# A deformable convolution's sampling stage on TensorE: transposes as products with the unit matrix, and every product on tiles of 64 columns

## The reference, cut to what matters

```python
def deform_conv2d(x, offset, weight, bias, pad=PAD):
    ...
    val = gather(y0, x0, (1 - dy) * (1 - dx)) + gather(y0, x0 + 1, (1 - dy) * dx) \
        + gather(y0 + 1, x0, dy * (1 - dx)) + gather(y0 + 1, x0 + 1, dy * dx)
    patches = val.reshape(Bx, C, KK, Hx, Wx)
    out = jnp.einsum('bikhw,oik->bohw', patches, weight.reshape(Cout, Cin, KK))
    return out + bias[None, :, None, None]
f_w = deform_conv2d(xr, off_w, w_dcnw, b_dcnw)
f_h = deform_conv2d(xr, off_h, w_dcnh, b_dcnh)
f_avg = (f_w + f_h).mean(axis=(2, 3), keepdims=True)
```

## Time and profile before

| what | before |
|---|---|
| median of 3 runs | 12,407.22 us |
| the profiled execution: time / span | 12,423.67 / 12,421.6 us |
| sampling stage on TensorE | 563 to 7,577 us of the span |
| TensorE busy in the span | 93% |
| VectorE, ScalarE, GpSimd busy in the span | 83%, 83%, 48% |

### The profile page before, as it was taken

One profiled execution on the slowest core, in us unless ns is written; L12 is line 12 of the kernel. 1 busy time (PEld: TensorE's weight loads), 2 busy tenths in 40 slices (PEclk: granted clock), 3 DMA queues, 4 the chain that ended last, 5 costly groups with the idle time before them and its releaser, 6 DMA issues. The chain is left out here.

```text
span 12421.6 us, 338253 instructions
## 1 busy us (share of the span) xinstructions
PE 11555.8 (93%) x133056; PEld 8928.9 (72%) x133056; DVE 10330.4 (83%) x13907; ACT 10361.2 (83%) x10330; POOL 5958.3 (48%) x3910
## 2 busy tenths in 40 slices
PE   7699999999999999999999999880699899999999
PEld 4599999999999999999999996430533355555555
DVE  5588888888888888888888886799878788888888
ACT  3499899899998998989989885397768899899988
POOL 0155554455444545445454451033300388888887
PEclk9899999999999999999999997895899899999999
DMA  6688888888888888888888888444644333333332
GB/s 181 164 209 206 208 205 203 204 206 208 204 204 201 208 206 207 206 200 208 206 207 205 202 206 210 140 155 139 178 130 159 127 99 108 102 100 107 99 103 85
DMA packets 850969, 2144.79 MB, mean 173 GB/s; under 512 B 108322, under 2 KB 447184, under 8 KB 707168
## 3 DMA queue, kind: packets, MB, share of 16 engines
q1 hardware_dynamic: 833904, 2090.65, 63.7%
q10 hardware_dynamic: 15120, 30.71, 0.7%
q0 software_dynamic: 384, 1.79, 0.0%
HBM read 1827.33 MB, written 295.56 MB: 171 GB/s over the span
## 5 line engine op out<-in xcount | busy, mean ns | idle before, releaser
L831 PE MATMUL dc_p<-dc_t 96*64 96x108 f32 x103896 | 5162.5, 257 | 85.9 <-issue 44.9
L831 PEld LDWEIGHTS dc_p<-dc_t 96*64 96x64 f32 x103896 | 4847.6, 136 | 353.6 <-issue 351.7
L900 POOL TENSOR_TENSOR dc_t<-dc_t 128x486 f32<-128x486 f32 x2885 | 3169.6, 1099 | 3525.6 <-DVEq L990 2344.8
L972 DVE TENSOR_TENSOR dc_t<-dc_p,dc_t 128x972 f32<-128x972 f32 x2886 | 3367.5, 1167 | 976.0 <-DVEq L970 880.4
L779 ACT ACTIVATE dc_t<-dc_t 96x2304 f32<-96x2304 f32 x1447 | 3191.8, 2206 | 222.3 <-ACTq L778 219.0
L784 ACT ACTIVATE dc_t<-dc_t 96x2304 f32<-96x2304 f32 x1446 | 3049.7, 2109 | 0.0
L2481 DVE TENSOR_TENSOR_SCAN ms_t<-ms_t,ms_p 128x512 f32<-128x512 f32 x1728 | 2128.5, 1271 | 282.9 <-PE ms_p L2423 203.5
L2397 POOL TENSOR_TENSOR ms_t<-ms_t 128x1536 f32<-128x1536 f32 x576 | 1987.9, 3457 | 503.5 <-DVE ms_t L2481 499.7
L2433 PE MATMUL ms_p<-ms_t,top_t 128*128 128x512 f32 x3456 | 1774.7, 596 | 0.0
L2423 PEld LDWEIGHTS ms_p<-top_t,ms_t 128*128 128x128 f32 x6912 | 849.7, 141 | 967.6 <-issue 693.1
L872 PE MATMUL dc_p<-dc_t 128*128 128x180 f32 (+1 forms) x7488 | 1537.0, 337 | 0.6 <-PEq L867 0.3
(11 more groups left out here) (256 smaller groups left out, 9864.2 us busy)
## 6 DMA issues: line engine op xcount, KB each, us to landing
dc_t<-sxd SPq DMA_DIRECT2D x1447, 864.0 KB, 5.9
ms_t<-bcd SPq DMA_DIRECT2D x576, 256.0 KB, 3.3
dc_t<-xrT SPq DMA_DIRECT2D x145, 540.0 KB, 9.0
kvd<-wk_t SPq DMA_DIRECT2D x18, 1536.0 KB, 5.1
szd<-mi_t SPq DMA_DIRECT2D x36, 768.0 KB, 4.4
xvd<-mi_t SPq DMA_DIRECT2D x36, 768.0 KB, 4.8
dld<-mi_t SPq DMA_DIRECT2D x36, 768.0 KB, 3.4
ms_t<-dld SPq DMA_DIRECT2D x36, 768.0 KB, 6.7
```

The source lines that it names most:

```text
L831: ins = e.matmul(PT[j % 2][o:o + 64, t // 3, (t % 3) * WIN * CG:(t % 3 + 1) * WIN * CG], HX[:, m // 2 % RP, m % 2, t * 128 + o:t * 128 + o ...
L900: e.tensor_tensor(ZH[:, n % 4, :, :], z[:, :, 0:HALF], z[:, :, HALF:2 * HALF], ALU.add)\
L972: e.tensor_tensor(Zt[:, n % 4, :].rearrange("p (b m i) -> p b m i", b=3, i=CG), PT[n % 2][:, :, 0:3 * WIN * CG].rearrange("p b (m i) -> p ...
```

## The change

Both transposes (L859, L840) become ordinary matmuls: the data is now the stationary operand, 64 columns at a time, at column 0 or 64 of the array, and the unit matrix (128 columns) is the moving one. The convolution's matmul (L872) is split into two of 64 stationary columns in the same way, each against the same 180 moving columns. So that 64 columns are always there, `VA` is padded from 1,620 to 1,664 columns (zeroed once) and `ACC` from 180 to 218; the transposed pieces of `ACC` are then 128 columns from 0 and from 90 (they were 90 from each), of which 90 rows are used as before. VectorE's two copies of the last three chunks become one.

```diff
-        VA = p.sb([128, 2, NG * LEN])
+        VA = p.sb([128, 2, NCK * 128])
-        ACC = p.sb([128, NRB, 2, CM])
+        ACC = p.sb([128, NRB, 2, CM + 38])
...
                 def turn_sum(i, conv):
                     for h in range(2):
-                        ins = e.transpose(PR[0:HM, (2 + h) * 128:(3 + h) * 128], ACC[:, i, conv, h * HM:(h + 1) * HM],
-                                          k.ident[:, :])
+                        for o in (0, 64):
+                            ins = e.matmul(PR[o:o + 64, (2 + h) * 128:(3 + h) * 128],
+                                           ACC[:, i, conv, h * HM + o:h * HM + o + 64], k.ident[:, :],
+                                           start=True, stop=True, tile_position=(0, o))
...
                         for u, c in enumerate(pieces[g]):
-                            o = min(128, NG * LEN - 128 * c)
-                            ins = e.transpose(PR[0:o, u * 128:(u + 1) * 128],
-                                              VA[:, n // NG % 2, 128 * c:128 * c + o], k.ident[:, :])
+                            for o in (0, 64):
+                                ins = e.matmul(PR[o:o + 64, u * 128:(u + 1) * 128],
+                                               VA[:, n // NG % 2, 128 * c + o:128 * c + o + 64], k.ident[:, :],
+                                               start=True, stop=True, tile_position=(0, o))
...
                         for u, c in enumerate(pieces[g]):
-                            o = min(128, NG * LEN - 128 * c)
-                            ins = e.matmul(PF[:, conv * CM:(conv + 1) * CM], VT[0:o, n // 2 % 2, u, :],
-                                           WD[0:o, c, conv, :], start=(c == 0), stop=(c == NCK - 1),
-                                           skip_group_check=True)
+                            kr = min(128, NG * LEN - 128 * c)
+                            for o in (0, 64):
+                                ins = e.matmul(PF[o:o + 64, conv * CM:(conv + 1) * CM], VT[0:kr, n // 2 % 2, u, o:o + 64],
+                                               WD[0:kr, c, conv, :], start=(c == 0), stop=(c == NCK - 1),
+                                               skip_group_check=True, tile_position=(0, o))
...
+                e.memset(VA[:, :, NG * LEN:NCK * 128], 0.0)
...
-                    full = sum(128 * (c + 1) <= NG * LEN for c in pieces[g])
-                    ins = e.tensor_copy(VT[:, n // 2 % 2, 0:full, :].rearrange("p u x -> p (u x)"), PR[:, 0:full * 128])
-                    if full < len(pieces[g]):
-                        o = NG * LEN % 128
-                        ins = e.tensor_copy(VT[0:o, n // 2 % 2, full, :], PR[0:o, full * 128:(full + 1) * 128])
-                    ins.then_inc(s_vt, 1)
+                    m = len(pieces[g])
+                    e.tensor_copy(VT[:, n // 2 % 2, 0:m, :].rearrange("p u x -> p (u x)"), PR[:, 0:m * 128]).then_inc(s_vt, 1)
```

More of the change, by code:

```diff
@@ L905, in keep @@
                     e.wait_ge(s_cr[i % 2], 32).then_inc(s_cr[i % 2], -32)
-                    e.tensor_scalar(ACC[:, i, :, :], ACC[:, i, :, :], KF[:, i:i + 1], None, ALU.mult).then_inc(s_pre, 1)
+                    e.tensor_scalar(ACC[:, i, :, 0:CM], ACC[:, i, :, 0:CM], KF[:, i:i + 1], None, ALU.mult).then_inc(s_pre, 1)
                     e.wait_ge(s_pre, 1).then_inc(s_pre, -1)
-                    e.tensor_tensor(ACC[:, i, :, :], ACC[:, i, :, :], CR[:, i, :].rearrange("p (v c) -> p v c", v=2),
+                    e.tensor_tensor(ACC[:, i, :, 0:CM], ACC[:, i, :, 0:CM], CR[:, i, :].rearrange("p (v c) -> p v c", v=2),
                                     ALU.add).then_inc(s_acc, 1)
@@ L943, in add_up @@
                         e.wait_ge(s_acc, 1).then_inc(s_acc, -1)
-                    a = ACC[:, i, conv, :]
+                    a = ACC[:, i, conv, 0:CM]
                     e.tensor_tensor(a, a, PF[:, conv * CM:(conv + 1) * CM], ALU.add).then_inc(s_ff, 1)
```

## The result

The changed kernel takes 12,567.8 us (median of 4 runs, 12,537.3 to 12,582.0) against 12,410.1 before: ratio 1.0125, 95% interval 1.0105 to 1.0145. It is slower by 1.25%. The forecast was 12,597, range 12,375 to 12,740. The profiled execution has a span of 12,564.9 us, 143 more than before. Of all executions in this document one is left out, of experiment 9's kernel, which took 25,148 us at a granted clock of 0.72 for 0.96 in the others; no run here shows why.

A forecast was written before the change was run, and what follows sets the result against it. TensorE's own stream was taken to bound the sampling stage. Switches -504, transposes +475, convolution 0, late code +219 and the rest 0 gave +190 us: 12,407 + 190 = 12,597 us, range 12,375 to 12,740.

The forecast's parts named there:

- What bounds it: Sampling stage: TensorE's own stream sets its end, busy 6,960.4 of 7,013.7 us, until ScalarE (10% slack) binds.
- Part 1: Pair step: gaps at changes of tiling, 0.35 us a step, all go: 504 us off.
- Parts 2 and 3: Transposes as products need two passes, 0.11 to 0.22 us each: +475 us; convolution's split matmuls run side by side: 0.
- C: Rival: the array still empties between 96 and 128 rows, part 1 gives nothing: 13,101 us, chance 0.07.
- D: Rival: weight loads of one tile wait for the other tile's matmul: 13,507 us, chance 0.03.
- Part 4: TensorE's code stream: 18% more instructions, packets last 6.23 us for 7.36, more come late, 101 us become 320: +219.
- Part 5: The rest: VectorE's dropped copy, later transposes, order of waits, padding and start of the next load: 0.
- A: Rival: code arrives in time, parts 1 to 3 alone, 12,378 us, or 12,396 with more packets; chance 0.25.
- B: Rival: the tail of late code grows less than threefold, 12,396 to 12,480 us; chance 0.20.

The follow-up runs named there:

- experiment 9: Convolution alone on 64-column tiles, transposes as before, loads split and paced, against the kernel before: 12,285.3 us, ratio 0.9893.
- Experiment 2: The convolution on tiles: kernel before with the convolution alone on 64-column tiles, transposes still 128 wide: 12,463.2 us, ratio 1.0033.
- experiment 1: The full-width products: kernel before with both transposes made ordinary unit-matrix products, 128 columns wide: 12,819.3 us, ratio 1.0322.
- experiment 4: Changed kernel with only the first half of each 864 KB load from the second loop body on: 12,317.0 us, ratio 0.9911 to the changed kernel.
- experiment 8: The shorter step: kernel before with sampling moving 102 columns for 108 at 3 of 9 taps, same code: 12,384.1 us, ratio 0.9974.
- Experiment 3: Kernel before with 26.4 semaphore instructions a pair step added to TensorE's stream, same matmuls and tiling: 13,554.0 us, ratio 1.0907.
- experiments 4 to 7: Data load halved in the changed kernel (12,317.0 us) and kernel before (12,330.2); load split and paced in the changed kernel (12,321.1) and kernel before (12,339.2).

## Why the prediction was right, point by point

- **What bounds it.** Right. TensorE's stream sets this stage: the stage grew by 154 us and the span by 143.
- **Part 1, the switches: -504.** Right in mechanism. Experiment 2 shows the gap moving with the change of tiling, experiment 1 shows it staying where the tiling stays. The loader's rows show it gone.
- **Parts 2 and 3: +475 and 0.** Right. Products cost 0.11 us more each, and split matmuls run side by side for the price of one. Parts 1 to 3 together: forecast -29, measured 1,440 x (4.783 - 4.800) = -24. The rule of the Trainium skill ("TensorE: Matmul & The Clock Gate", section "The mechanism", not the one after it that the forecast names), by which a load overlaps a running matmul only where the row groups differ, is not borne out: in experiment 4 the loader is idle for 0.3 us in all before the convolution's 14,976 loads and for 0.4 us before those of the products at L864. Rivals C and D fall.
- **Part 4, late code: +219.** Right in what it is, late code, and a fifth too large: +178. The loss grew 2.8-fold and the waits 3.0-fold, where 3.2 was forecast. That it came so near is in part luck. The same formula (a tail that falls by e in 0.98 us, moved by the change in a packet's time) gives a loss of some 79 us for the full-width products, 111 for the shorter step and 168 for the convolution on tiles; measured were 3, 151 and 213. It ascribes all to the time that a packet lasts. Experiments 1 and 8 show that the step's length counts by itself: 59 ns less added 54 us, and 337 ns more took all but 3 us away. The changed step is 17 ns shorter; at experiment 8's rate of 0.9 us for a nanosecond that is some 15 of the 178 us (an estimate). The other 160 are put down to the larger code by difference. The nearest comparison is between experiments 8 and 2: with 10.4 loads and matmuls more in a step, and a step 13 ns longer, the loss is 213 us for 151. Experiment 3, meant to show it directly, did not. What the packets are up against was named in the forecast only as "the transfers it must pass"; experiments 4 to 7 name it: one 864 KB load a step, which a packet must wait out. "Runtime: NRT & Kernel Launch" of the Trainium skill, section "Instruction fetch mechanics", calls the crossing of a block mostly hidden. That holds for all but 146 of the 1,098 packets in the stage; these cost 275 us, 2.2% of this program.
- **Part 5: 0.** Right: VectorE's waits at its sampling line are 860.1 us for 859.7. Its copies' waits for the transposes rose from 8.7 to 25.0 us, with no effect on the end of the stage that shows beside the late code.
- **Rivals.** A (code in time) was wrong as the kernel stood. With the paced load it comes true, and 12,321 is even below its 12,378 to 12,396, since most of the 97 us lost before go as well. B's range ended below the result.

## What to carry to other kernels

A stall of TensorE that waits for no semaphore, and that lies a whole number of code packets after the last such stall, was late code each time here: count the loads and matmuls between two such stalls before you look for a data dependency. Price an edit by its instructions as well as by its array time when the engine's stream is straight-line code of some hundred instructions in 5 us. And if one large load fills the DMA engines for most of a step, split it and send its second half later: the two edits together were worth 0.7% before the change and 2% after it.

## What the runs showed of the hardware that I had not expected

- Two 64-column tiles need not start in step: one ran a matmul ahead of the other across three kinds of work, and nothing was lost by it (a quiet step of 4.783 us, as in experiment 4, where the stretch shown has them in step).
- A code packet started only as a data load drained, and TensorE went on 2.3 to 3.0 us after the start of a packet that was late.
- A longer array step makes code arrive in time: with 0.34 us more in a step, TensorE's waits for code went from 46 to 2.
- 26 semaphore instructions a step in TensorE's stream cost 0.6 us in the median step and 1,130 us in all.
